# Reordering the last matrix product of a two-layer graph convolution, with its layer norms and its last bucket sums

## Chip, core and metric

One core of a Trainium2 chip. The metric is device time in microseconds (us), the median of several runs. TensorE (PE) does the matrix products, VectorE (DVE) and ScalarE (ACT) the elementwise work, GpSimd (POOL) issues the row gathers, SyncE (SP) all other transfers.

## What is computed

x is 1250 x 768; there are 21250 edges (src, dst) with one of 8 types.

```
def _rgcn_conv(x, src, dst, etype, W, root, b):
    seg = dst * num_rel + etype
    sums = segment_sum(x[src], seg)
    cnt = segment_sum(ones, seg)
    mean = (sums / maximum(cnt, 1.0)[:, None]).reshape(num_nodes, num_rel, -1)
    return einsum('nri,rio->no', mean, W) + x @ root + b

h = relu(_rgcn_conv(x, ..., W1, root1, b1))
x = layernorm(x + _rgcn_conv(h, ..., W2, root2, b2))      # eps 1e-5
```

## The kernel before

The 1250 nodes are ten **tiles** of 125 rows (T = 10). Output columns come in two **halves** of 384 (HALF). One matrix product over all nodes is called a matrix; it has 20 **steps** (STEPS), one per tile and half. A step is 18 matmuls (L720): six slices of the inner dimension times three, because each float32 operand is split into a high and a low part (high*high, high*low, low*high). In all matrices `h, t = divmod(s, T)` (L729): steps 0 to 9 do the left half of tiles 0 to 9, steps 10 to 19 the right half.

In a layer, seven relations are multiplied first and aggregated afterwards: their products go to DRAM (`y`), rows are gathered by edge (L474, POOL) and summed per destination by a matmul with a one-hot matrix (L747). A **bucket** is what the edges of one relation give for one tile of destinations; its gathered blocks are split by ACT into `g_high` (L586, L589) and by DVE into `g_low` (L986, L989), DVE builds the one-hot matrices (L978), PE multiplies, and DVE adds the result to `acc` (L997, L999). The eighth relation is averaged first and then multiplied (matrix MEAN1 in layer 1, MEAN2 in layer 2).

The change touches MEAN2, the last matrix, and what runs beside it:

- **PE** (L925, through `matrix`, L876): in each step the 18 matmuls into one of four banks (L734, after waiting for the bank: `kept`, L843), then the bucket sums that `actions(s)` names. In MEAN2 these are the ten buckets of the last relation, placed by `last_sums` (L300): tile t is summed after step 3 + 15*t//9, that is 3, 4, 6, 8, 9, 11, 13, 14, 16, 18. A bucket there is 14 matmuls, over four gathered blocks. After step 2 PE, ACT and DVE read a count of spilled edges and branch on it (L773, L665, L1053).
- **DVE** (L1356, through `matrix`, L1011): in step s it adds the product to `acc` (`keep_mean2`, L1341, operation L967); if the step has a sum, it first prepares the *next* bucket (four one-hot matrices, three `g_low`, one folded piece of 64 partitions that goes to `g_high`: L978, L986) and then adds the bucket that PE sums after this step (L997). Only bucket 0 is prepared earlier, at step 2. From step 10 on `layer_norm` (L1345) follows: statistics of tile s - 10 (L1349 to L1351), and for the tile before it the reciprocal (L1337) and the normalisation of 768 columns, `(acc - mean) * 1/std` (L1338).
- **ACT** (L701): the `g_high` of the next bucket (four of 768 columns, L586), and from step 11 on the square root of one tile's variance (`deviation`, L697), one step behind DVE's statistics.
- **POOL**: gathers of the last relation (L566). Gather i is issued when block i - 5 has been split by DVE (`low_ready`, L473), since there are five buffers `raw`. ACT writes a `g_high` slot once PE has used the block four before it (L583).
- **SP** (L423): waits for `normed` tile by tile and sends each tile of `acc` to the output (375 KiB each); nothing else is left on its queue then.

Within an engine everything is in program order, so the steps above are a schedule written out by hand.

Of the kernel before, what the change touches and what calls it, by code (L numbers as in the profile page):

```python
# [8 lines left out]
def rgcn_residual_layernorm(nc, x, src, dst, etype, w_all, b1, b2, out):  # L9
# [21 lines left out]
    R = Q // 2 - 1  # L31
    P = 128
    K = D // P
    HALF = D // 2
    T = -(-N // P)
# [31 lines left out]
    STEPS = 2 * T  # L67
# [14 lines left out]
    with ctx:  # L82
        def sb(name, shape, dt=f32):
            return ctx.enter_context(nc.sbuf_tensor(name, shape, dt))

        def sem(name):
            return ctx.enter_context(nc.semaphore(name))
# [31 lines left out]
        stats = sb("stats", [P, 2, 2, 6])  # L119
        moments = sb("moments", [P, 2, 2])  # L120
        std = sb("std", [P, 2, 2])
        spill_n = sb("spill_n", [P, 1], i32)
        spill_index = sb("spill_index", [P, 1], i32)
        spill_gid = sb("spill_gid", [P, 1])
# [97 lines left out]
        var_ready = sem("var_ready")  # L222
        std_ready = sem("std_ready")
        normed = sem("normed")
        out_stored = sem("out_stored")
        spill_copied = [sem(f"spill_copied{l}") for l in range(2)]
        spill_shifted = [sem(f"spill_shifted{l}") for l in range(2)]
# [13 lines left out]

        def unit(q, h):
            return 2 * q + h

        def behind(g):

# [42 lines left out]
        def averaging(g, r, n):  # L289
# [7 lines left out]
                return todo  # L297
            return actions

        def last_sums(g):  # L300
            return lambda s: [("sum", g, R - 1, t) for t in range(T) if s == 3 + (STEPS - 5) * t // (T - 1)]

        def sums_behind(g, s):
            return sum(len(last_sums(g)(n)) for n in range(s))
# [20 lines left out]
        def banks(shift, turning=False):  # L325
            return lambda s: 2 + s % 2 if turning and s >= T else (s + shift) % BANKS
# [5 lines left out]
        def _(sp):  # L332
# [88 lines left out]
            with sp.Fori(2, R) as r:  # L421
                relation(r + ROOT2 - 1, stored_before(1, r), r)
            for t in range(T):  # L423
                sp.wait_ge(normed, t + 1)
                sp.dma_start(out[t * NT:t * NT + ROWS[t], :], acc[0:ROWS[t], t, :]).then_inc(out_stored, 16)
            sp.wait_ge(out_stored, 16 * T)

# [142 lines left out]
        def _(act):  # L570
# [54 lines left out]
            def matrix(q, yc, bank, actions=lambda s: [], more=True, spilled=None, ahead=False, high_at=1, after=None):  # L625


                cut = SPILL_STEP[spilled[0]] if spilled else -1
                order = [(s, a) for s in range(STEPS) for a in actions(s) if a[0] != "turn"]
                ready = n = 0  # L630
                for s in range(STEPS):
                    sums = sum(a[0] != "turn" for a in actions(s))
                    turns = [a for a in actions(s) if a[0] == "turn"]
                    n += sums
                    if not ahead or ready == 0:
                        for m in range(ready, n):
                            bucket(order[m][1][1], order[m][1][3])
                        ready = n
                    if yc is not None:
                        stage_y(yc, STEPS * q + s, s, bank(s))  # L640
                    for _, turn, _, t in turns:
                        if turn == 2:
                            relu(t)
                    if ahead and sums:

                        last = min(n + 1, len(order))
                        last -= last > n and s <= cut < order[n][0]
                        for m in range(ready, last):
                            bucket(order[m][1][1], order[m][1][3])
                        ready = last  # L650
                    for _, turn, _, t in turns:
                        high_of_turn(turn, t)
                    for what, g, _, t in actions(s):
                        if what == "average":
                            average(g, t)
                    if s == high_at:
                        high_of_unit(q, 1)
                    if s == 11 and more:
                        high_of_unit(q + 1, 0)
                    if s == cut:  # L660
                        high_spilled(*spilled)
                    if after:
                        after(s)
# [33 lines left out]
            def deviation(t):  # L697
                act.wait_ge(var_ready, t + 1)
                act.activation(std[:, t % 2, 0:1], moments[:, t % 2, 1:2], ACT.Sqrt, bias=eps[:]).then_inc(std_ready, 1)

            matrix(MEAN2, None, None, finishing, more=False, spilled=(1, 2 * R - 1), ahead=True, high_at=0,  # L701
                   after=lambda s: deviation(s - T - 1) if s > T else None)
            deviation(T - 1)


        @block.tensor
        def _(pe):
# [18 lines left out]
                pe.wait_ge(w_low_ready, unit(q, h) + 1)  # L726

            def step(q, s, bank, free):
                h, t = divmod(s, T)  # L729
                if t == 0:  # L730
                    unit_ready(q, h)
                for wait in free:
                    pe.wait_ge(*wait)
                product(q, h, t, bank).then_inc(prod_done, 1)  # L734
# [108 lines left out]
            def kept(base, before, n=None, turning=False):  # L843


                def free(s):
                    wait = [(h_low_ready, 2 * T * n + 2 * s + 2)] if n is not None and s < T else []
                    if s < 2 and n is not None:
                        return wait + [(before[0], before[1] - 1 + s)]
                    if s < BANKS:  # L850
                        return wait + [(h_low_ready, 2 * T * (n + 1))]
                    return wait + [(root_kept, base + s + 1 - (2 if turning and s >= T else BANKS))]
                return free
# [76 lines left out]
        def _(dve):  # L930
# [401 lines left out]
            matrix(MEAN2 - 1, averaging(2 * R - 3, R - 2, 3), low_at=in_parts)  # L1332


            def norm(t):
                dve.wait_ge(std_ready, t + 1)
                link(dve.reciprocal(std[:, t % 2, 1:2], std[:, t % 2, 0:1]))  # L1337
                dve.tensor_scalar(acc[:, t, :], acc[:, t, :], moments[:, t % 2, 0:1], std[:, t % 2, 1:2],  # L1338
                                  ALU.subtract, ALU.mult).then_inc(normed, 1)

            def keep_mean2(s):  # L1341
                dve.wait_ge(bucket_added, 2 + T * (2 * R - 1) + sums_behind(2 * R - 1, s))
                keep(STEPS * MEAN2 + s, s % T, s // T, banks(2)(s), plus="acc")

            def layer_norm(s):  # L1345
                t = s - T
                if t >= 0:
                    dve.wait_ge(root_kept, 3 * STEPS + s + 1)
                    dve.bn_stats(stats[:, t % 2, 0, :], acc[:, t, 0:HALF])  # L1349
                    link(dve.bn_stats(stats[:, t % 2, 1, :], acc[:, t, HALF:D]))  # L1350
                    dve.bn_aggr(moments[:, t % 2, :], stats[:, t % 2].rearrange("p c s -> p (c s)"))\  # L1351
                        .then_inc(var_ready, 1)
                if t >= 1:
                    norm(t - 1)

            matrix(MEAN2, finishing, keep_mean2, more=False, spilled=(1, 2 * R - 1), after=layer_norm,  # L1356
                   low_at=((1, 0, K),))
            norm(T - 1)


# [20 lines left out]
```

## Time and profile before

| what | value |
|---|---|
| median of 3 runs | 1575.47 us (1573.15 to 1580.7) |
| profiled execution, own time | 1582.24 us |
| its span, first to last instruction | 1580.4 us |
| mean granted clock of TensorE | 0.976 |
| first matmul of MEAN2's step 3 | 1482.09 us |
| last instruction of DVE | ends 1571.14 us |

The span is the part of the profiled execution that the trace covers; all times below are counted from its start. PEld is the weight load of TensorE, which overlaps its matmuls. An arrow in brackets names what ended the idle time before an instruction.

### The profile page before, as it was taken

Reading aid. Unit: us, or ns where it says so; the run is one execution under the profiler, and the core shown is the slowest. Engines: PE = TensorE matmul, PEld = TensorE weight load, DVE = VectorE, ACT = ScalarE, POOL = GpSimd, SP = SyncE. Lnnn points to the kernel's source line nnn. Section 1 sums busy time; section 2 is a strip of 40 time slices with the busy share of each in tenths; the row PEclk is TensorE's granted clock in tenths of the full one; section 3 lists DMA queues with packets and bytes.
Section 4 is the critical chain, followed back from the end, with each engine's and each line's share of the span. In section 5 each row is a group of like instructions: output and inputs, shape, how many; then the busy total and the mean of one; then the engine's idle time right before and its main releaser. Section 6 shows DMA issues by size and latency. Waiting matters only on the chain.

```text
span 1580.4 us, 23799 instructions
## 1 busy us (share of the span) xinstructions
PE 1485.0 (94%) x9014; PEld 1462.6 (93%) x9014; DVE 1022.3 (65%) x1599; ACT 572.7 (36%) x818; POOL 629.2 (40%) x455
## 2 busy tenths in 40 slices
PE   6999998999999998999989799999999999899995
PEld 5999998999999998998989799999999999899995
DVE  6899999955777765885971022545454545478797
ACT  3222111112444543584552111333333334258542
POOL 1121112223677774664620310434343424366561
PEclk9999999999999998999999899999999999999998
DMA  4353221243677766765423441656565555576443
GB/s 163 114 189 123 83 74 34 71 140 112 190 245 218 215 206 210 221 201 160 142 85 130 150 149 42 197 157 203 167 197 172 190 182 184 171 234 202 137 138 124
DMA packets 102645, 249.79 MB, mean 158 GB/s; under 512 B 12607, under 2 KB 75758, under 8 KB 102486
## 3 DMA queue, kind: packets, MB, share of 16 engines
q0 software_dynamic: 31680, 131.81, 27.5%
q1 hardware_dynamic: 70870, 116.69, 22.2%
q8 instruction: 62, 1.02, 0.3%
q14 instruction: 33, 0.27, 0.0%
HBM read 204.47 MB, written 65.49 MB: 171 GB/s over the span
## 4 chain that ended last, share of the span: by engine, by line
PE 58%; DVE 20%; DMA 12%; POOL 4%; issue 3%; ACT 2%; SPq 0%; DVEq 0%; ACTq 0%; POOLq 0%
PE prod L720 45%; PE agg L747 11%; DMA y<-y_stage 5%; DMA raw<-y,bucket_index 5%; DVE slot_hot L1214 3%; POOL raw L474 2%; DVE ranks L1169 2%; DVE ranks L1164 2%; DVE keyed L1222 2%; POOL scale L482 1%; DVE dst_hot L1215 1%; DVE g_low L989 1%; PE prod L711 1%; DMA x_rows<-in_x 1%; DVE g_low L986 1%
## 5 line engine op out<-in xcount | busy, mean ns | idle before, releaser
L720 PE MATMUL prod<-w_high,h_high 128*128 128x384 f32 x2160 | 736.3, 341 | 20.2 <-ACT y_stage L622 12.8
L720 PE MATMUL prod<-w_low,h_high 128*128 128x384 f32 x2160 | 730.4, 338 | 0.0
L720 PE MATMUL prod<-w_high,h_low 128*128 128x384 f32 x2160 | 729.7, 338 | 0.0
L474 POOL DMA_INDIRECT raw<-y,bucket_index x380 | 492.8, 1297 | 559.5 <-DVE g_low L989 296.8
L989 DVE TENSOR_TENSOR g_low<-raw,g_high 128x768 fp32r<-128x768 f32 x280 | 259.1, 954 | 306.6 <-ACT g_high L589 305.8
L720 PEld LDWEIGHTS prod<-w_high,h_high 128*128 128x128 f32 x2160 | 412.3, 191 | 22.8 <-ACT y_stage L622 15.4
L720 PEld LDWEIGHTS prod<-w_low,h_high 128*128 128x128 f32 x2160 | 411.8, 191 | 0.0
L720 PEld LDWEIGHTS prod<-w_high,h_low 128*128 128x128 f32 x2160 | 411.5, 191 | 0.0
L622 ACT ACTIVATE y_stage<-prod 128x384 f32<-128x384 f32 x280 | 137.5, 492 | 702.4 <-PE prod L720 639.7
L589 ACT ACTIVATE g_high<-raw 128x768 fp32r<-128x768 f32 x300 | 243.2, 842 | 106.8 <-DMA raw<-y,bucket_index 87.6
L747 PE MATMUL agg<-g_high,one_hot 128*128 128x384 f32 x760 | 202.5, 348 | 22.6 <-DVE g_low L989 20.6
L747 PE MATMUL agg<-g_low,one_hot 128*128 128x384 f32 x680 | 176.2, 341 | 0.0
L747 PEld LDWEIGHTS agg<-g_high,one_hot 128*128 128x128 f32 x760 | 135.9, 190 | 33.5 <-issue 17.5
L461 POOL TENSOR_TENSOR w_low<-w_raw,w_high 128x2304 fp32r<-128x2304 f32 x8 | 58.7, 7341 | 252.4 <-ACT w_high L576 252.4
L747 PEld LDWEIGHTS agg<-g_low,one_hot 128*128 128x128 f32 x680 | 126.3, 191 | 0.0
L999 DVE SCALAR_TENSOR_TENSOR acc<-agg,inv_count,acc 128x768 f32<-128x768 f32 x120 | 121.3, 1011 | 4.4 <-PE agg L747 4.1
L945 DVE TENSOR_TENSOR w_low<-w_raw,w_high 128x2304 fp32r<-128x2304 f32 (+1 forms) x37 | 72.7, 1965 | 56.5 <-ACT w_high L576 56.5
L576 ACT ACTIVATE w_high<-w_raw 128x2304 fp32r<-128x2304 f32 x36 | 76.5, 2125 | 64.5 <-PE prod L720 46.6
L586 ACT ACTIVATE g_high<-raw,scale 128x768 fp32r<-128x768 f32 x80 | 70.8, 931 | 72.3 <-issue 39.4
L978 DVE TENSOR_SCALAR one_hot<-column,dst_local 128x128 fp32r<-128x128 bf16 x380 | 89.0, 290 | 7.5 <-issue 7.0
L967 DVE TENSOR_TENSOR acc<-prod,acc 128x384 f32<-128x384 f32 x60 | 33.2, 554 | 82.5 <-PE prod L720 81.8
L1214 DVE TENSOR_SCALAR slot_hot<-slot,edge_f 125x512 f16<-125x512 f16 x170 | 60.6, 430 | 0.0
(138 smaller groups left out, 772.1 us busy)
## 6 DMA issues: line engine op xcount, KB each, us to landing
y<-y_stage SPq DMA_DIRECT2D x280, 187.5 KB
w_raw<-in_w_all SPq DMA_DIRECT2D x36, 1152.0 KB
raw<-y,bucket_index POOLq DMA_INDIRECT x380, 5.3
x_rows<-in_x SPq DMA_DIRECT2D x10, 375.0 KB
y<-in_x SPq DMA_DIRECT2D x1, 3750.0 KB, 14.8
y<-acc SPq DMA_DIRECT2D x10, 375.0 KB
acc<-in_x SPq DMA_DIRECT2D x10, 375.0 KB
out<-acc SPq DMA_DIRECT2D x10, 375.0 KB
```

What stands on the lines that cost most here:

```text
L474: pool.indirect_dma_start(raw[:, i % NRAW, :], None, y[0:written * N, :], bass.IndirectOffsetOnAxis(ap=bucket_index[:, at_column:at_column ...
L576: act.activation(w_high[:, h], w_raw[:], ACT.Copy).then_inc(w_high_ready, 1)
L586: act.activation(g_high[:, split_slot(g, i), :], raw[:, slot, :], ACT.Copy, scale=scale[:, i:i + 1])\
L589: act.activation(g_high[:, split_slot(g, i), :], raw[:, slot, :], ACT.Copy).then_inc(high_ready, 1)
L622: act.activation(y_stage[:, s % BANKS, :], prod[:, bank, 0:HALF], ACT.Copy)\
L720: mm = pe.matmul(prod[:, bank, 0:HALF], left[:, k, t * P:(t + 1) * P], right[:, h, k, :], start=(k == 0 and left is h_high and right is w_ ...
L747: mm = pe.matmul(agg[:, par, c, 0:HALF], one_hot[:, par, b, :], part[:, split_slot(g, i), c * HALF:(c + 1) * HALF], start=(b == 0 and part ...
L945: ins = dve.tensor_tensor(w_low[:, h, part], w_raw[:, part], w_high[:, h, part].bitcast(f32), ALU.subtract)
L978: ins = dve.tensor_scalar(one_hot[:, par, b, :], column[:], dst_local[:, bass.ds(column_of(r, t, b), 1)], None, ALU.is_equal)
L989: ins = dve.tensor_tensor(low[p:P, split_slot(g, i), :], rows, high, ALU.subtract)
L999: ins = dve.scalar_tensor_tensor(a, agg[:, t % 2, :, 0:HALF], inv_count[:, bass.ds(r * T + t, 1)], a, ALU.mult, ALU.add)
L1214: dve.tensor_scalar(slot_hot[:, c % 2, j, :], slot[0:EP, :], place[:, e:e + 1], None, ALU.is_equal)
```

## The change

MEAN2 no longer does all left halves first. With LEAD = 4: steps 0 to 3 are the left halves of tiles 0 to 3, steps 4 to 7 their right halves, and from step 8 on the halves of one tile follow each other. The bucket sums of the last relation move to steps 4 + 13*t//9, which are 4, 5, 6, 8, 9, 11, 12, 14, 15, 17 (the same relation in layer 1 keeps its steps). A tile is finished at the later of its second half and its sum: steps 4, 5, 6, 8, 9, 11, 13, 15, 17, 19 for tiles 0 to 9. DVE takes the statistics in that step. ACT takes the square root in the same step (before: one step later). In the next step DVE, ahead of its addition of the product, waits for the square root, takes the reciprocal and computes `shift = -mean/std` (128 x 1), and ACT, behind its `g_high`, normalises the tile with `Identity(acc * 1/std + shift)`. Tile 9 is still normalised by DVE, under a semaphore of its own.

```
         def part_of(q, s):
+            if not (isinstance(q, int) and q == MEAN2):
+                return divmod(s, T)
+            if s < 2 * LEAD:
+                return divmod(s, LEAD)
+            return s % 2, s // 2
+
+        def finished_at(t):
+            return max(LEAD + t if t < LEAD else 2 * t + 1, last_sum_at(2 * R - 1, t))
+
+        def finished(s):
+            return [t for t in range(T) if finished_at(t) == s]
...
+        def last_sum_at(g, t):
+            first, steps = (3, STEPS - 5) if g < R else (4, 13)
+            return first + steps * t // (T - 1)
+
         def last_sums(g):
-            return lambda s: [("sum", g, R - 1, t) for t in range(T) if s == 3 + (STEPS - 5) * t // (T - 1)]
+            return lambda s: [("sum", g, R - 1, t) for t in range(T) if s == last_sum_at(g, t)]
...
-                sp.wait_ge(normed, t + 1)
+                sp.wait_ge(*((normed, t + 1) if t < T - 1 else (last_normed, 1)))
...
+            def norm(t):
+                act.wait_ge(norm_ready, t + 1)
+                act.activation(acc[:, t, :], acc[:, t, :], ACT.Identity, bias=shift[:, t % 2, :],
+                               scale=std[:, t % 2, 1:2]).then_inc(normed, 1)
+
+            def layer_norm(s):
+                for t in finished(s - 1):
+                    norm(t)
+                for t in finished(s):
+                    deviation(t)
+
             matrix(MEAN2, None, None, finishing, more=False, spilled=(1, 2 * R - 1), ahead=True, high_at=0,
-                   after=lambda s: deviation(s - T - 1) if s > T else None)
-            deviation(T - 1)
+                   after=layer_norm)
...
-                h, t = divmod(s, T)
+                h, t = part_of(q, s)
...
-                    wait = [(h_low_ready, 2 * T * n + 2 * s + 2)] if n is not None and s < T else []
+                    h, t = part_of(MEAN2 if n == 3 else None, s)
+                    wait = [(h_low_ready, 2 * T * n + 2 * t + 2)] if n is not None and h == 0 else []
...
-            def norm(t):
+            def scale_of(t):
                 dve.wait_ge(std_ready, t + 1)
                 link(dve.reciprocal(std[:, t % 2, 1:2], std[:, t % 2, 0:1]))
-                dve.tensor_scalar(acc[:, t, :], acc[:, t, :], moments[:, t % 2, 0:1], std[:, t % 2, 1:2],
-                                  ALU.subtract, ALU.mult).then_inc(normed, 1)
+                dve.tensor_scalar(shift[:, t % 2, :], moments[:, t % 2, 0:1], std[:, t % 2, 1:2], -1.0,
+                                  ALU.mult, ALU.mult).then_inc(norm_ready, 1)

             def keep_mean2(s):
+                for t in finished(s - 1):
+                    scale_of(t)
+                h, t = part_of(MEAN2, s)
                 dve.wait_ge(bucket_added, 2 + T * (2 * R - 1) + sums_behind(2 * R - 1, s))
-                keep(STEPS * MEAN2 + s, s % T, s // T, banks(2)(s), plus="acc")
-
-            def layer_norm(s):
-                t = s - T
-                if t >= 0:
+                keep(STEPS * MEAN2 + s, t, h, banks(2)(s), plus="acc")
+
+            def moments_of(s):
+                for t in finished(s):
                     dve.wait_ge(root_kept, 3 * STEPS + s + 1)
+                    dve.wait_ge(bucket_added, 2 + T * (2 * R - 1) + t + 1)
                     dve.bn_stats(stats[:, t % 2, 0, :], acc[:, t, 0:HALF])
                     link(dve.bn_stats(stats[:, t % 2, 1, :], acc[:, t, HALF:D]))
                     dve.bn_aggr(moments[:, t % 2, :], stats[:, t % 2].rearrange("p c s -> p (c s)"))\
                         .then_inc(var_ready, 1)
-                if t >= 1:
-                    norm(t - 1)
...
-            norm(T - 1)
+            last = (T - 1) % 2
+            dve.wait_ge(std_ready, T)
+            link(dve.reciprocal(std[:, last, 1:2], std[:, last, 0:1]))
+            dve.tensor_scalar(acc[:, T - 1, :], acc[:, T - 1, :], moments[:, last, 0:1], std[:, last, 1:2],
+                              ALU.subtract, ALU.mult).then_inc(last_normed, 1)
```

## Rows read from the trace of the kernel before

**Rows 1.** The page: PE's busy time, and the chain that ended last by engine.
```profile
PE 1485.0 (94%) x9014; PEld 1462.6 (93%) x9014; DVE 1022.3 (65%) x1599; ACT 572.7 (36%) x818; POOL 629.2 (40%) x455
...
PE 58%; DVE 20%; DMA 12%; POOL 4%; issue 3%; ACT 2%; SPq 0%; DVEq 0%; ACTq 0%; POOLq 0%
```

**Rows 2.** Busy time by stretch: length, then PE, PEld, DVE, ACT, POOL, clock, DMA.
```profile
1540.00:1550.00 10.00, 9.93 (x58) 9.61 (x57) 9.84 (x19) 3.83 (x5) 6.92 (x6) 1.00 0.60 176
...
1560.00:1570.00 10.00, 2.90 (x17) 2.58 (x15) 9.61 (x25) 1.18 (x4) 0.00 (x0) 0.85 0.28 97
```

**Rows 3.** Chain of waits, MEAN2 steps 3 and 4 (start, us, what).
```profile
1479.65 2.44 issue
1482.09 4.79 PE prod L720 x18
1486.88 2.46 PE agg L747 x14
1489.35 3.12 PE prod L720 x18
```

**Rows 4.** Timeline of DVE, one full step (start, us, what), and bucket 1's start.
```profile
1487.47 0.94 DVE L978 TENSOR_SCALAR one_hot<-column,dst_local 128x128 fp32r<-128x128 bf16 x4
...
1543.42 0.55 DVE L967 TENSOR_TENSOR acc<-prod,acc 128x384 f32<-128x384 f32 x1
1543.88 0.86 DVE L978 TENSOR_SCALAR one_hot<-column,dst_local 128x128 fp32r<-128x128 bf16 x4
1544.67 2.87 DVE L986 SCALAR_TENSOR_TENSOR g_low<-raw,scale,g_high 128x768 fp32r<-128x768 f32 x3
1547.57 1.02 DVE L986 SCALAR_TENSOR_TENSOR g_high<-raw,scale,g_high 64x768 fp32r<-64x768 f32 x1
1548.62 0.96 DVE L997 TENSOR_TENSOR acc<-agg,acc 128x768 f32<-128x768 f32 x1
1549.49 0.55 DVE L1349 BATCH_NORM_STATS2 stats<-acc 128x6 f32<-128x384 f32 x1
...
1550.54 0.21 DVE L1351 BATCH_NORM_AGGREGATE moments<-stats 128x2 f32<-128x12 f32 x1
1550.66 0.11 DVE L1337 RECIPROCAL std<-std 128x1 f32<-128x1 f32 x1
1550.81 0.68 DVE L1338 TENSOR_SCALAR acc<-acc,moments,std 128x768 f32<-128x768 f32 x1
1551.40 0.55 DVE L967 TENSOR_TENSOR acc<-prod,acc 128x384 f32<-128x384 f32 x1
```

**Rows 5.** Waits, 1460 to 1581: us in total, times, longest.
```profile
DVE g_low L986 <- ACT g_high L586: 1.1, 5, 0.3
```

**Rows 6.** Timeline of ACT: its square roots and what stands around them.
```profile
1528.47 1.28 ACT L699 ACT_TABLE_LOAD   x1
1529.76 0.30 ACT L699 ACTIVATE std<-moments,eps 128x1 f32<-128x1 f32 x1
...
1533.68 3.42 ACT L586 ACTIVATE g_high<-raw,scale 128x768 fp32r<-128x768 f32 x4 [1.08 <-PE agg L747]
...
1567.15 0.29 ACT L699 ACTIVATE std<-moments,eps 128x1 f32<-128x1 f32 x1 [3.07 <-DVE moments L1351]
```

**Rows 7.** Timelines: PE's last matmul; DVE's last statistics and last norm.
```profile
1562.56 0.34 PE L720 MATMUL prod<-w_high,h_low 128*128 128x384 f32 x1
...
1569.41 0.21 DVE L1351 BATCH_NORM_AGGREGATE moments<-stats 128x2 f32<-128x12 f32 x1
...
1570.46 0.68 DVE L1338 TENSOR_SCALAR acc<-acc,moments,std 128x768 f32<-128x768 f32 x1
```

**Rows 8.** By stretch, columns as in rows 2; the last is GB/s.
```profile
1563.00:1564.00 1.00, 0.00 (x0) 0.00 (x0) 0.93 (x5) 0.22 (x1) 0.00 (x0) 1.00 0.33 77
...
1567.00:1578.00 11.00, 0.00 (x0) 0.00 (x0) 3.97 (x11) 0.59 (x2) 0.00 (x0) 0.50 0.32 127
...
1579.00:1580.40 1.40, 0.00 (x0) 0.00 (x0) 0.00 (x0) 0.00 (x0) 0.00 (x0) 0.50 0.02 9
```

More of the change, by code:

```diff
@@ L121, in rgcn_residual_layernorm @@
         std = sb("std", [P, 2, 2])
+        shift = sb("shift", [P, 2, 1])
         spill_n = sb("spill_n", [P, 1], i32)
@@ L224, in rgcn_residual_layernorm @@
         normed = sem("normed")
+        last_normed = sem("last_normed")
+        norm_ready = sem("norm_ready")
         out_stored = sem("out_stored")
@@ L243, in unit, with part_of @@
             return 2 * q + h
+        LEAD = 4
+        def part_of(q, s):
+            if not (isinstance(q, int) and q == MEAN2):
[7 more added lines that the diff above has]
+            return [t for t in range(T) if finished_at(t) == s]
         def behind(g):
@@ L1352, in layer_norm @@
                         .then_inc(var_ready, 1)
-                if t >= 1:
-                    norm(t - 1)
-            matrix(MEAN2, finishing, keep_mean2, more=False, spilled=(1, 2 * R - 1), after=layer_norm,
+            matrix(MEAN2, finishing, keep_mean2, more=False, spilled=(1, 2 * R - 1), after=moments_of,
                    low_at=((1, 0, K),))
-            norm(T - 1)
+            last = (T - 1) % 2
[3 more added lines that the diff above has]
+                              ALU.subtract, ALU.mult).then_inc(last_normed, 1)
 def kernel(x, src, dst, edge_type_8, L0_gnn_W1, L0_gnn_root1, L0_gnn_b1, L0_gnn_W2, L0_gnn_root2, L0_gnn_b2):
```

## The prediction

> **What bounds the kernel now.** I read the page first. PE is busy for 94% of the span and carries 58% of the chain that ended last [rows 1]. The change touches only the last matrix, so at most the stretch from step 3 on, some 98 us of 1580, can move. There I read busy time by stretch. Around 1545 us PE and DVE are both full (9.93 and 9.84 of 10 us), and after 1560 us PE runs out of work (2.90) while DVE goes on (9.61) [rows 2]. PE's last matmul ends at 1562.90, DVE's last norm at 1571.14 [rows 7]. So the end is set by DVE, 8.2 us behind PE, and then by a tail of transfers: 1580.40 - 1571.14 = 9.26 us. The timeline of DVE shows why: a step with both a bucket and a norm takes 7.98 us from one addition of a product to the next [rows 4], while PE needs 3.12 for the product and 2.46 for the bucket, together 5.58 [rows 3].
>
> **PE's own work** doesn't change: the same products and buckets, in another order. If nothing held it, then from the end of step 3's product at 1486.88 [rows 3] it would need 16 products and ten buckets: 16 x 3.12 + 10 x 2.46 = 74.5, ending at 1561.4. That is the floor, and it is little better than the 1562.9 of now.
>
> **The price list of DVE**, by the distances between starts [rows 4]: addition of a product 0.46 (alone about 0.6), one-hot matrices 0.79, three g_low 2.90, folded piece 1.05, addition of a bucket 0.87, statistics 1.05 + 0.12, reciprocal 0.15, norm 0.59.
>
> **The norm moves to ACT.** DVE loses 0.59 per tile and gets a 128 x 1 operation; the trace has none of this kind with two operands, the nearest row is the reciprocal with 0.15 [rows 4], bounds 0.05 and 0.3. But the order adds a wait. Before, the square root of a tile was one step old when DVE asked for it. Now DVE asks at once after the statistics, and nothing stands between. Behind that wait stand DVE's addition of the next product and all the preparation of the next bucket. The square root starts when the moments are out and takes 0.29 [rows 6]; with a hop each way I take 0.36, bounds 0.29 and 0.6. So a full step goes from 7.98 to 7.98 - 0.59 + 0.15 + 0.36 = 7.90. **Nearly all that DVE gives away comes back as a wait.** ACT itself has room: 3.83 of 10 us busy [rows 2], and a norm there should cost about what a g_high of the same size costs (3.42 for four, [rows 6]), so under 1 us, bounds 0.8 and 1.1, beside DVE's g_low work.
>
> **The table load.** It stands before the first square root, 1.28 us [rows 6]. Now it came at 1528.47 while nobody waited. With tile 0 finished in step 4 it falls into the wait just described, unless it is issued ahead of it: bounds 0 and 1.28, taken 1.28, because the load stands under the line of the square root, behind its wait. The square root follows the load at once, at 1529.76 [rows 6]. The Trainium skill (ScalarE: Activation LUTs, What ACT_TABLE_LOAD costs) puts a drain of about 1.38 us beside the load; by it the end would be another 1.4 us later. The row shows no such gap before the square root.
>
> **The sums move.** The first bucket goes from step 3 to step 4. Before, DVE began bucket 1 at 1487.47, right behind step 3's product [rows 4]; now it has nothing to do until step 4's product, 1486.88 + 3.12 = 1490.0. That gives away 2.5 us of the engine that is the bound. From there DVE's order is fixed. Up to the last piece that bucket 8 needs (prepared in step 14) it does six full steps (4, 5, 6, 8, 9, 11): 47.4; step 12 without statistics: 0.46 + 0.79 + 2.90 + 1.05 + 0.87 = 6.07; steps 7 and 10, an addition each: 1.2; step 13, addition and statistics with their wait: 0.6 + 1.83 = 2.43; step 14 up to the fold: 5.20. Together 62.3. To this come the table load 1.28 and waits for g_high: 1.1 us over five now [rows 5]; ACT now starts a bucket only after the square root, so I take 0.8, bounds 0 and 2.4. Sum 64.4, so 1554.4. PE's work meanwhile (products 5 to 15, buckets 0 to 7) is 54.0, so PE is the one that waits.
>
> **The end of the chain goes back to PE.** Bucket 8 ends about 0.4 later, at 1554.8. Then products 16 and 17, 6.24: 1561.0. Bucket 9, already prepared: 1563.5. Products 18 and 19: 1569.7. Then addition 0.6, statistics 1.05, aggregate 0.21, square root 0.36, reciprocal 0.15, norm 0.68, together 3.0: **1572.8**, which is 1.6 later than now. DVE's backlog of today is gone, but PE ends 6.8 later than today.
>
> **The output tail shrinks.** Now the last tile leaves behind others: the moved rate is 127 GB/s from 1567 to 1578 [rows 8], so at 1571.14 some 0.98 MB were still to go, two and a half tiles of 0.384 MB. After the change ACT's norm of tile 8 comes at about 1568.2 (bucket 9 at 1563.5, its addition, statistics, square root, norm), 4.6 us ahead of tile 9, so tile 9 has the queue to itself. One transfer alone moves 77 GB/s [rows 8], which makes 5.0 us; with a start of under 1 us and the 1 us in which almost nothing moves at the end (9 GB/s, [rows 8]) I take 6.6, bounds 5.0 (at 127 GB/s) and 9.26. Gain 2.7. The first eight outputs move earlier too (the first to about 1504: step 4's 7.9 us after 1490, the table load, the g_high of step 5 and a norm, instead of 1533), in among the gathers; nothing is queued behind them on SP. I cost them at nothing: four of them already share the engines with gathers now (DMA share 0.60, [rows 2]). Without this cover they would lengthen gathers, which is a rival below. The wait for h_low moves with the tile and costs nothing: all turns are done before step 2.
>
> **The sum:** 1572.8 + 6.6 = 1579.4 against 1580.4, a gain of 1.0. The profiled execution took 1582.24, so it would take 1581.2; it stood 6.8 above the median of the three runs, and I subtract from that median: **1574.5 us**. A measurement of this kernel tells about 0.5%, 7.9 us, from no change, so the forecast is no measurable difference. From the bounds above: the small operation and the square root, on eight tiles, -1.4 to +3.1; table load -1.3; g_high waits -0.8 to +1.6; tail -1.6 to +2.7.
>
> **Rivals.**
>
> *DVE is really relieved.* If neither the wait for the square root nor the late start mattered, PE would run through: 1561.4 + 3.0 + 6.6 = 1571.0, a gain of 9.4, 1566.1 us. For it: DVE's total falls, and its eight full-width norms go. Against: the 7.90 of a full step stand against PE's 5.58, and four of the five steps 4 to 8 are such steps. To reach it DVE would have to be 7 us or more shorter. Chance 0.06.
>
> *Gathers get late.* The outputs from 1504 us on take part of the DMA engines while POOL's gathers need them, and each bucket's chain starts with a gather that waited for DVE. If each of the six buckets behind the first output got 1 us later and nothing absorbed it, the time would be 1580.5. For it: the DMA share is already 0.60 [rows 2]. Against: a gather's five buffers run a bucket ahead and ACT is idle 6 us in 10. Chance 0.12; still within 0.5%.
>
> *The square root and the scaling don't share a table.* Identity is not in the trace of before; if it needed another table than the square root, ACT would load at each change of function. DVE waits for the load before a square root, on tiles 1 to 6 and on tile 9: 7 x 1.28 = 9.0, ending at 1583.5, 8.0 slower than now. It decides from the second tile on, in step 5. For it: nothing beyond that the case is not shown. Against: the copy with a scale at 1533.68 follows a square root with no load [rows 6]. Chance 0.03. The Trainium skill (ScalarE: Activation LUTs, Table sets: the hidden batching unit) says that cheap functions, identity among them, are in every set; by it this rival falls.
>
> *The clock.* A gap of 2.44 us at 1479.65 is followed by a product of 4.79 instead of 3.12 [rows 3]. If DVE's longer steps open such a gap in PE, each costs up to 1.7. I expect PE's gaps in pieces under 1 us; chance 0.05 for one or two of them, 1577.
>
> **How the numbers follow.** Forecast 0.74, gathers 0.12, relieved DVE 0.06, clock 0.05, table 0.03. Around the forecast the bounds reach some 5 us either way. The range 1568 to 1580.5 takes in the forecast's bounds, the clock and the gathers' case, and leaves out most of the other two. Faster by over 0.5% (below 1567.6): the relieved DVE and a little of the forecast's low end, 0.07. Slower by over 0.5% (above 1583.3): the table rival and a part of the late gathers, 0.05. Within: 0.88.
>
> **What would show it.** Right: DVE's step with bucket and norm still near 7.9 us, with about 0.36 idle before each reciprocal that ends with ACT's square root; one table load near step 4 with DVE idle 1.5 or more; DVE idle 2.5 before step 4's addition; PE waiting for g_low in most buckets; PE's last matmul near 1570 and 3 us from there to the last norm; a tail near 6.6. Wrong: PE's last matmul before 1565 (DVE was relieved); more than two table loads; ACT waiting for gathers while DVE waits for ACT's g_high; a tail still near 9.

## The result, and the profile after

| | median us | ratio to before, 95% interval |
|---|---|---|
| before | 1577.12 | |
| changed | 1588.36 (1583.16 to 1592.6, 6 runs) | 1.0064, 1.0033 to 1.0095 |
| changed, 12 more runs, later | 1589.88 | 1.0064, 1.0042 to 1.0086 |

The last row stands beside 1579.45 for the kernel before on the same chip. The change makes the kernel 10 us slower. I had forecast no difference, 1574.5 us, with 1580.5 as the upper end of the range. One of the 12 executions of a kernel below (e4) ran at a mean granted clock of 0.79 and took 1743.68 us; it stands in no ratio.

The profiled execution of the changed kernel has a span of 1581.4 us, 1.0 longer than that of before. Single executions of one kernel differ by several us ahead of the last matrix: over all 20 profiles of this study its step 3 begins between 1475.9 and 1489.9 us. So I compare the **last stage**, from the start of step 3's product to the end of the span. The page after (busy time; the chain by engine):

```profile
PE 1484.4 (94%) x9014; PEld 1460.1 (92%) x9014; DVE 1021.0 (65%) x1599; ACT 579.7 (37%) x827; POOL 626.8 (40%) x455
...
PE 60%; DVE 19%; DMA 14%; issue 3%; ACT 2%; POOL 2%; SPq 0%; DVEq 0%; ACTq 0%; POOLq 0%
```

The chain of waits of the changed kernel in that stage (start, us, what):

```profile
1478.70 6.50 PE prod L754 x36
1485.20 2.49 PE agg L781 x14
...
1499.46 7.43 DMA raw<-y,bucket_index
...
1528.34 6.51 DMA raw<-y,bucket_index
...
1544.28 7.68 DMA raw<-y,bucket_index
...
1555.72 6.27 PE prod L754 x36
1561.99 2.48 PE agg L781 x14
1564.47 6.26 PE prod L754 x36
```

Steps 3 and 4 lie back to back, then the chain leaves PE and runs over DVE, ACT and gathers of 6.5 to 7.7 us, and from 1555.72 on it is PE again: two products, bucket 9, two products, as predicted.

The timeline of DVE, one step with bucket and norm, as [rows 4]:

```profile
1521.99 0.55 DVE L1002 TENSOR_TENSOR acc<-prod,acc 128x384 f32<-128x384 f32 x1
1522.45 0.86 DVE L1013 TENSOR_SCALAR one_hot<-column,dst_local 128x128 fp32r<-128x128 bf16 x4
1523.24 2.87 DVE L1021 SCALAR_TENSOR_TENSOR g_low<-raw,scale,g_high 128x768 fp32r<-128x768 f32 x3
1526.14 1.02 DVE L1021 SCALAR_TENSOR_TENSOR g_high<-raw,scale,g_high 64x768 fp32r<-64x768 f32 x1
1527.19 0.96 DVE L1032 TENSOR_TENSOR acc<-agg,acc 128x768 f32<-128x768 f32 x1
1528.25 0.56 DVE L1387 BATCH_NORM_STATS2 stats<-acc 128x6 f32<-128x384 f32 x1
...
1529.31 0.21 DVE L1389 BATCH_NORM_AGGREGATE moments<-stats 128x2 f32<-128x12 f32 x1
1529.88 0.16 DVE L1372 RECIPROCAL std<-std 128x1 f32<-128x1 f32 x1 [0.36 <-ACT std L723]
1530.08 0.21 DVE L1373 TENSOR_SCALAR shift<-moments,std 128x1 f32<-128x1 f32 x1
1530.21 1.01 DVE L1002 TENSOR_TENSOR acc<-prod,acc 128x384 f32<-128x384 f32 x2
```

From one addition to the next it is 8.22 us, against 7.98 before: the wait of 0.36 stands ahead of the reciprocal, reciprocal and shift take 0.33 together, and the statistics begin 1.06 behind the start of the bucket's addition instead of 0.87, since they now need the sum just made. (Where they need an older sum, for tile 7 at 1563.97, it is 0.87 in this kernel too.)

The waits from 1460 us on, as [rows 5] (total, times, longest):

```profile
ACT g_high L610 <- DMA raw<-y,bucket_index: 15.0, 9, 3.3
PE agg L781 <- DVE g_low L1021: 8.5, 7, 2.4
DVE g_low L1021 <- ACT g_high L610: 5.4, 8, 1.4
...
DVE std L1372 <- ACT std L723: 3.3, 9, 0.4
...
DVE g_high L1021 <- ACT g_high L610: 1.8, 1, 1.8
```

The timeline of ACT, as [rows 6]: the table load runs ahead of the wait of the square root it serves (it ends at 1491.59, the square root is released at 1494.44), so it costs nothing.

```profile
1490.31 1.28 ACT L723 ACT_TABLE_LOAD   x1
1494.44 0.30 ACT L723 ACTIVATE std<-moments,eps 128x1 f32<-128x1 f32 x1 [2.84 <-DVE moments L1389]
...
1497.95 1.02 ACT L727 ACTIVATE acc<-acc,shift,std 128x768 f32<-128x768 f32 x1
```

And DVE's last instruction, as [rows 7] (the span ends at 1581.4):

```profile
1573.24 0.68 DVE L1397 TENSOR_SCALAR acc<-acc,moments,std 128x768 f32<-128x768 f32 x1
```

Counted from the start of step 3's product, so that the kernels can be laid beside each other (worked out from the timelines, one profile each, two where two numbers stand; the tail is the time from the end of the last norm to the end of the span):

| kernel | PE's last matmul | last norm | tail | stage |
|---|---|---|---|---|
| before | 80.8 / 79.5 | 89.1 / 87.8 | 9.3 / 9.2 | 98.3 / 97.0 |
| forecast | 87.6 | 90.7 | 6.6 | 97.3 |
| changed | 92.0 / 91.6 | 95.2 / 94.8 | 7.4 / 6.6 | 102.7 / 101.4 |

One part of these stages has nothing to do with the schedule. From the start of step 3's product to the start of what follows, PE takes 3.2 us in 16 of the 20 profiles, and 4.6 to 5.9 in the other four: the first one of before, and below the two kernels with the sums at 3 (a2, f1) and b2. The granted clock of TensorE is lower there. By stretch, columns as in [rows 2], first before, then changed:

```profile
1482.10:1485.10 3.00, 3.00 (x9) 3.00 (x10) 2.97 (x4) 1.61 (x2) 1.69 (x2) 0.50 0.50 135
```
```profile
1478.90:1481.90 3.00, 3.00 (x18) 3.00 (x18) 2.26 (x4) 1.67 (x2) 2.39 (x3) 1.00 0.31 86
```

Behind this product the stage takes 93.7 and 93.8 us before and 99.4 and 98.1 changed; the forecast comes to 92.7. So the stage loses 4.4 us from its start, or 5.7 and 4.4 behind the product. That is about half of the 10 that the times show; the experiments had to find both parts.

### The profile page after: what moved, and what is told of

Its sections match the earlier page's. It is cut to its first block, busy times and chain, and to the rows that moved or that the text cites. A ratio compares the mean times of both kernels' runs of the same rounds, so it can differ in the third digit from the quotient of the medians.

```text
span 1581.4 us, 23818 instructions
## 1 busy us (share of the span) xinstructions
PE 1484.4 (94%) x9014; PEld 1460.1 (92%) x9014; DVE 1021.0 (65%) x1599; ACT 579.7 (37%) x827; POOL 626.8 (40%) x455
## 3 DMA queue, kind: packets, MB, share of 16 engines
q8 instruction: 62, 1.02, 0.3%
## 4 chain that ended last, share of the span: by engine, by line
PE 60%; DVE 19%; DMA 14%; issue 3%; ACT 2%; POOL 2%; SPq 0%; DVEq 0%; ACTq 0%; POOLq 0%
PE prod L754 47%; PE agg L781 11%; DMA y<-y_stage 6%; DMA raw<-y,bucket_index 5%; DVE slot_hot L1249 3%; DMA x_rows<-in_x 2%; DVE ranks L1204 2%; DVE ranks L1199 2%; DVE keyed L1257 2%; DVE g_low L1021 2%; DVE dst_hot L1250 1%; DVE g_low L1024 1%; POOL raw L498 1%; PE prod L745 1%; DVE ranks L1191 1%
## 5 line engine op out<-in xcount | busy, mean ns | idle before, releaser
L613 ACT ACTIVATE g_high<-raw 128x768 fp32r<-128x768 f32 x300 | 242.2, 841 | 96.9 <-DMA raw<-y,bucket_index 79.2
L1021 DVE SCALAR_TENSOR_TENSOR g_low<-raw,scale,g_high 128x768 fp32r<-128x768 f32 x60 | 58.2, 1014 | 8.3 <-ACT g_high L610 8.3
```

Source lines behind the costliest of these rows:

```text
L613: act.activation(g_high[:, split_slot(g, i), :], raw[:, slot, :], ACT.Copy).then_inc(high_ready, 1)
L1021: ins = dve.scalar_tensor_tensor(low[p:P, split_slot(g, i), :], rows, scale[p:P, i:i + 1], high, ALU.mult, ALU.subtract)
```

## The experiments

Each kernel ran 12 times (the held outputs 11) beside 23 to 35 executions of the kernel before on the same chip. The ratio of one kernel to before is told to about 0.2%, 3 us; the difference of two such ratios only to about 0.3%, 5 us. *Stage* is counted from the start of step 3's product, *behind the product* from the start of what follows it. Each run has a short name, in brackets where it is introduced; in front of each result stands what I expected, as put down before the run.

### Where in the schedule

**The changed kernel again** (a0).

> The changed kernel once more, for a second profile and more times. All theories expect some 10 us over the kernel before, since its six times lay there. What it tells apart: the one profile of the changed kernel (1583.16 us) was its fastest run, and in it the last stage (from step 3's product to the end) had 102.7 us against 98.3 before. If the loss is made in the last stage and varies with the gathers, this profile shows a stage nearer 105 to 108 us with longer waits of DVE for ScalarE's g_high; if it is made elsewhere, the stage is again near 103 us and the span is longer ahead of it.

Measured: 1.0064 (1.0042 to 1.0086), stage 101.4. The waits repeat (DVE for g_high 4.8 us, nine waits of 0.36). The stage is not near 105, so the profiles leave some 5 us of the loss unexplained.

**Outputs held back** (a1).

```
             for t in range(T):
+                if t == 0:
+                    sp.wait_ge(normed, 5)
```

> Changed kernel, but SyncE sends no output before tile 4 is normalised (about where the kernel before sent its first one). Theory contention (the early outputs make gathers late): the waits of DVE for g_high (5.4 us in the profile of the changed kernel) fall to about 1 us and the time falls by 4 us or more. Theory schedule (DVE's late start, the wait for the square root and PE's end cause the loss): no change of the waits, time within 1 us of the changed kernel, or up to 3 us longer because more outputs queue at the end.

Measured: 1.0068 (1.0046 to 1.0091), stage 106.7. The first output leaves at 1532.09, and DVE waits longer for g_high, not less:

```profile
ACT g_high L612 <- DMA raw<-y,bucket_index: 17.2, 9, 4.8
DVE g_low L1023 <- ACT g_high L612: 9.4, 8, 4.0
```

PE's last matmul comes at 93.8, the tail grows to 9.6. Contention of the early outputs with the gathers falls as the cause of the waits and of the loss.

**The two parts of the schedule**, undone one at a time: the sums stay at steps 3 + 15t//9 (a2); or `scale_of`, which waits for the square root, moves behind DVE's addition and its bucket work (a3, "asks later"):

```
-            first, steps = (3, STEPS - 5) if g < R else (4, 13)
+            first, steps = (3, STEPS - 5)
```
```
             def keep_mean2(s):
-                for t in finished(s - 1):
-                    scale_of(t)
...
             def moments_of(s):
+                for t in finished(s - 1):
+                    scale_of(t)
```

> Changed kernel, but the last bucket sums stay at the steps of before (3 + 15t//9). Theory schedule: DVE starts bucket 1 one product (3 us) earlier and three full steps in a row fall apart, so 4 to 5 us faster than the changed kernel. Theory contention: the outputs still leave among the gathers, so at most 1 to 2 us faster.

> Changed kernel, but DVE asks for the square root at the end of the next step (after its bucket work) and not ahead of its next addition, so that nothing waits for ScalarE's square root. Theory schedule: the nine waits of 0.36 us go, 2 to 3 us faster. Theory contention: outputs leave 7 us later each, otherwise the same; no more than 1 us.

Measured, sums at 3: 1.0012 (0.9991 to 1.0033), stage 97.3. Asks later: 1.0027 (1.0002 to 1.0052), stage 96.9. Against 1.0064 that is some 8 and 6 us, each told to about 5, where I had expected 4 to 5 and 2 to 3. The stages gain 4.7 and 5.1; behind the product they take 92.5 and 93.7, against 93.7 of before. So either repair brings the stage back to that of before. The time with the sums at 3 is not clear of no change, the other is just clear of it. That hints at a loss outside the stage, and no more than hints.

### What lies outside the stage

**The kernel before again** (b0).

> The kernel before once more, for a second profile of it. In its first profile step 3 of the last matrix began at 1482.1 us and the stage from there to the end took 98.3; the changed kernel and its three variants began it at 1477.6 to 1485.7 and took 102.7 and 101.4 (changed kernel, two profiles), 106.7, 97.4 and 96.9. If the whole loss lies in the last stage, this profile begins the stage within that band and takes 95 to 98. If some 5 us are lost ahead of it, the stage begins at 1474 to 1477 here.

Measured: 1.0007 (0.9987 to 1.0027), stage 97.0 from 1482.8 on. So the starts in the profiles don't show a loss ahead of the stage.

**Only the new tile and the two semaphores, unused, in the kernel before** (b1):

```
         std = sb("std", [P, 2, 2])
+        shift = sb("shift", [P, 2, 1])
...
         normed = sem("normed")
+        last_normed = sem("last_normed")
+        norm_ready = sem("norm_ready")
```

> The kernel before with only the new tile (shift, 8 bytes per partition) and the two new semaphores, unused. Theory schedule: no change, within 2 us of before. Rival, layout: the new tile moves every tile behind it and the semaphores their numbers; if that costs time anywhere in the 1480 us ahead, this one is 4 us or more slower than before.

Measured: 1.0043 (1.0023 to 1.0064), 6.8 us, for a program that does nothing new. **The theory of the schedule alone falls.** Split in two, only the tile (d1) and only the semaphores (d2):

> The kernel before with only the new tile of 8 bytes, unused. The tile and the two semaphores together cost 0.43% (6.8 us). If the tile does it (it moves the small tiles behind it by 8 bytes; the large region stays where it was, since its start is rounded up), 5 to 7 us slower than before; if the semaphores do it, no change.

> The kernel before with only the two new semaphores, unused, in the middle of the list. If the semaphores' numbers do it, 5 to 7 us slower than before; if the tile does it, no change. If both of these two runs show no change, the 6.8 us were chance or need both.

Measured: tile 1.0033 (1.0014 to 1.0053), semaphores 0.9994 (0.9973 to 1.0015). It is the tile. Its 8 bytes per partition move the ten small tiles allocated behind it; by the sizes in the code, packed one behind another, the large region with `acc`, `raw`, `g_high` and `g_low` keeps its place. Two more unused tiles tell something about which places matter: 64 bytes instead of 8 (e2), and the 8 bytes further back, ahead of `small` (e4).

> The kernel before with an unused tile of 64 bytes instead of 8 in the same place, so that every tile behind it keeps its address modulo 64. If the 8 bytes cost because they put later tiles off an alignment, no change; if any shift costs (or what sits at the end of the memory), 5 us slower as with 8 bytes.

> The kernel before with the unused 8 bytes placed later, ahead of the tile 'small', so that only small, small_bf and over_bf move. If these are the tiles that mind, 5 us slower as with the tile in its place; if the edge tiles (payload, position, dl_bf, key_bf) do, no change.

Measured, 64 bytes: 1.0013 (0.9988 to 1.0038), which is not clear of no change, nor of the 8 bytes' effect (by the same sizes this one moves the large region too, by 64 bytes). 8 bytes ahead of `small`, moving only `small`, `small_bf` and `over_bf`: 1.0034 (1.0009 to 1.0059). So moving these three tiles is enough. **What in it costs is open**: they are used only in the first 430 us, where each DVE operation on them takes the same in either layout within what one layout varies by itself, and step 3 of the last matrix begins at 1482.4 on average over ten profiles without the 8 bytes and at 1483.0 over ten with them, each scattering by over 3. A part may lie in the last stage, where none of the three is used: behind step 3's product it takes 95.8, 95.7 and 95.6 us in the kernels with the unused 8 bytes, 93.7 and 93.8 in before and 94.7 with only the semaphores, one profile each. But with the 64 bytes it takes 95.4.

### The schedule without the tile's cost

The tile goes behind all others, and the semaphores to the end of the list (cut, the semaphores are left out):

```
-        shift = sb("shift", [P, 2, 1])
...
         base = -(-top // 32) * 32
+        shift = sb("shift", [P, 2, 1])
```

This is the changed kernel in that form (d3):

> The changed kernel, all of its schedule, but the new tile is placed behind all others and the new semaphores at the end of the list, so that everything of before keeps its place. Theory layout plus schedule: 5 us or more faster than the changed kernel, 3 to 5 us slower than before, which is what the last stage shows in the profiles (102.7 and 101.4 us against 98.3 and 97.0). Theory schedule alone: still 10 us slower than before.

Measured: 1.0038 (1.0017 to 1.0058). The schedule costs 6 us; the rest, 4 us between 1.0064 and 1.0038, is not told from nothing by this pair alone. PE waits 9.3 us for g_low, and DVE 4.7 us for the g_high that its g_low needs, as in the changed kernel.

And its two parts undone as above, one at a time (f1, f2) and both (e1):

> Changed kernel with the last sums at their steps of before and the tiles in their old places; DVE still waits for the square root. In the new layout it stood 0.12% over before (last stage 97.3 us), so with the tile's 0.3% gone 3 us faster than before; both repairs together gave 0.33% faster in the old layout. If it lies near 0, the wait for the square root is worth 3 to 5 us by itself.

> Changed kernel with the square root asked for later and the tiles in their old places; the sums stay at steps 4 + 13t//9. In the new layout it stood 0.27% over before (last stage 96.9 us), so with the tile's 0.3% gone 0 to 1 us faster than before. If it lies as low as both repairs together (0.33% faster), the move of the sums costs only where DVE also waits for the square root.

> Changed kernel with both repairs (last sums at their steps of before, square root asked for later) and the old places of all tiles. Its last stage was 96.0 us with the new layout, against 97 to 99 for the kernel before; with the tile's 5 us gone it should be 1 to 3 us faster than before, which five rounds may not tell from nothing. If it is still 3 us or more slower, the layout is not what the earlier run of it paid.

| schedule, old places | ratio | 95% interval | last norm | stage | behind the product |
|---|---|---|---|---|---|
| as changed (d3) | 1.0038 | 1.0017 to 1.0058 | 98.5 | 104.7 | 101.5 |
| sums at 3 (f1) | 1.0006 | 0.9991 to 1.0021 | 92.2 | 98.4 | 92.5 |
| asks later (f2) | 1.0010 | 0.9992 to 1.0028 | 91.1 | 97.6 | 94.3 |
| both (e1) | 0.9967 | 0.9949 to 0.9985 | 88.1 | 94.6 | 91.4 |

The stage of d3 is 2.0 us longer than the changed kernel's for a reason of its own: bucket 8 and the product behind it take 9.6 us there against 7.7, and the granted clock from 1557.4 to 1564.0 us is 0.57.

In these times the two losses add up: 0.32% and 0.28% alone, 0.71% together. With both repaired **the kernel is 0.33% faster than before**, 5 us, the best of this study. Its timeline of DVE has no wait ahead of a reciprocal except tile 9's. At 1511.62, in a step without a bucket:

```profile
1510.00 0.55 DVE L1387 BATCH_NORM_STATS2 stats<-acc 128x6 f32<-128x384 f32 x1
...
1511.05 0.21 DVE L1389 BATCH_NORM_AGGREGATE moments<-stats 128x2 f32<-128x12 f32 x1
1511.18 0.51 DVE L1002 TENSOR_TENSOR acc<-prod,acc 128x384 f32<-128x384 f32 x1
1511.62 0.16 DVE L1372 RECIPROCAL std<-std 128x1 f32<-128x1 f32 x1
1511.82 0.22 DVE L1373 TENSOR_SCALAR shift<-moments,std 128x1 f32<-128x1 f32 x1
```

The square root now runs beside the next addition, and in a step with a bucket beside the bucket work too. What the repairs did not take away are DVE's waits for g_high: 5.6 us, against 5.4 and 4.8 in the changed kernel. What fell are PE's waits for g_low, from 9.3 in d3:

```profile
DVE g_low L1021 <- ACT g_high L610: 5.6, 8, 1.7
...
PE agg L781 <- DVE g_low L1021: 2.9, 2, 2.4
```

The same schedule as e1 with the tile in its new place (b2):

> Changed kernel with both repairs: last sums at their steps of before, and DVE asking for the square root one step's work later. Measured alone they gave 8.9 and 6.4 us. If they are two losses that add up, 1575 or less and faster than before; if both act on the same thing (buckets too close together for their gathers), about 1580, no faster than the better one alone.

Measured: 1.0018 (0.9996 to 1.0041), stage 96.0. Beside e1 it is the tile that keeps this kernel from being faster than before. It does not explain why the repairs fail to add up here, 0.52% and 0.37% alone and 0.46% together, since the tile has the same place in all four. Behind the product they overlap in both layouts: 9.0 and 7.1 us alone against 10.1 together in the old places, 6.3 and 5.1 against 7.6 in the new. **Whether these are two losses or partly one is not settled.**

Four schedules have now run with the tile in both places. The new place costs 0.26% (as changed), 0.06% (sums at 3), 0.17% (asks later) and 0.51% (both), on average 0.25%.

### One part at a time

**Only the order of the product** (b3): sums at 3, and DVE normalises as before.

> Only the order of the product and of the layer norms is changed: last sums at the steps of before, DVE normalises all 768 columns itself one step behind. Against b2 it shows what the norm on ScalarE is worth when nothing waits for it: 9 x 0.59 less 9 x 0.3, about 2.5 us, so this one 2 to 3 us slower than b2. Against before it shows what the order is worth: layer norms of early tiles beside PE's work, 3 to 5 us faster if DVE is the bound of the stage.

Measured: 1.0025 (1.0004 to 1.0047) with the tile in its new place, stage 96.1, last norm 88.9, tail 7.2. Against b2 (1.0018) the times tell no worth of the norm on ScalarE. Behind the product the stage takes 92.9 here and 91.2 in b2, 1.7 us for it, in one profile each; from the stage's start it was hidden by b2's slow first product.

**Only the sums moved** (c1), in the kernel before.

> The kernel before with only the last bucket sums moved to steps 4 + 13t//9; product order, norms and layout as before. Theory schedule: DVE starts bucket 1 a product later and PE's end comes behind two products after the last bucket, so 3 to 5 us slower, with the last stage at 101 to 103 us. If the sums cost only together with the norms in the same steps, no change here.

Measured: 1.0019 (1.0000 to 1.0038), stage 98.3, last norm 88.6. Behind the product the profile shows a loss of 1.3 us (95.1 against 93.7 and 93.8, but 94.7 with only the semaphores added), the times perhaps 3: moved alone, the sums cost little. I put that down to the norms, which here still stand in steps 10 to 19; no run shows it.

**Only the norm on ScalarE** (e3), in the old places.

> Old product order, old steps of the sums, old places of the tiles; only the norm goes to ScalarE, with its wait for the square root ahead of DVE's next addition, as in the changed kernel. Theory schedule: what DVE gives (0.59 a tile) it gets back in waits (0.36 + 0.33 measured for the two small operations and the hop), so last stage within 1 us of before, less 2 to 3 us at the end since the outputs queue no longer.

Measured: 1.0014 (0.9994 to 1.0033), no change that can be told. PE's last matmul comes at 84.7 instead of 80.8, the last norm at 92.8 instead of 89.1, and the tail is 7.5 instead of 9.3. So the last norm is about 4 us later in this profile, and the shorter queue of outputs gives half of it back. But most of the 4 us is one wait for g_high, and ACT stood idle for a gather then (timelines of DVE and of ACT):

```profile
1551.58 1.02 DVE L1017 SCALAR_TENSOR_TENSOR g_low<-raw,scale,g_high 128x768 fp32r<-128x768 f32 x1 [3.30 <-ACT g_high L606]
```
```profile
1550.62 1.76 ACT L606 ACTIVATE g_high<-raw,scale 128x768 fp32r<-128x768 f32 x2 [3.38 <-DMA raw<-y,bucket_index]
```

Whether the norm on ScalarE made that gather late is not shown.

## Why the prediction was wrong

**It missed a rival.** I listed four ways for it to go and none was the new tile itself. Its declaration, the first line that the change adds to the kernel, was read as costing nothing and was not priced at all. It costs 0.33 to 0.43% in the three kernels that have an unused tile and no new work, some 5 to 7 us, and 0.06 to 0.51% in the four schedules. With it alone added, my forecast would have been about 1580, and the measured 1588 would still lie above.

**The term of the sum that was mis-sized is DVE's stretch from step 4's addition to the last piece of bucket 8.** I had 64.4; it was 69.8 (1485.31 to 1555.07 in the changed kernel). The other terms moved the stage less: its start -1.3 (step 3's product ran at the higher clock), PE's end +0.4, the last norm +0.1, the tail +0.8; together they make the 5.4 between 97.3 and 102.7. The stretch by its parts:

- *The full step:* 7.90 forecast, 8.22 measured where nothing else waits, six times 0.3, about 2. The wait of 0.36 was right. What I missed is that the statistics now wait for the sum of the same step (0.19), and that with nothing behind it the aggregate counts with its whole 0.21 instead of 0.12.
- *Waits for g_high:* 0.8 forecast, bounds up to 2.4; about 4.5 measured in this stretch, of the 5.4 in the whole stage. This is the largest part, 3.7 us. I took them from five waits of before [rows 5], and that profile was the lowest of all: the nine profiles in which DVE does the norm have 1.1 to 3.9 us of them ahead of `g_low` in the stage, the eleven with the norm on ScalarE 3.5 to 5.9, and 9.4 with the outputs held. So the price was too low even for kernels without the hand-over. ACT in turn waits for gathers (11.7 us in the stage, 15.0 from 1460 on), and POOL issues a gather only when DVE has split the block five before it.
- *The table load:* 1.28 forecast, 0 measured; the load stands ahead of the wait. The Trainium skill's drain of 1.38 us beside the load (ScalarE: Activation LUTs, What ACT_TABLE_LOAD costs) can't be seen here either: ACT was idle for 2.84 us behind it, which would hide one.
- *A first step of 9.8* instead of 7.9: 0.9 of it are waits for g_high, counted above (ScalarE's second g_high of bucket 1 had to wait 0.77 for PE's bucket 0), and 0.48 is a wait ahead of the first statistics.

**What held.** DVE is the bound in the middle, and what the norm gave it comes back as the round trip (0.59 against 0.36 and 0.33); the end goes to PE, two products, a bucket, two products: 15.3 forecast, 15.7 measured from bucket 8's last piece; last norm 3.2 behind PE instead of 3.0; the tail 6.6 forecast, 7.4 and 6.6 measured, against 9.26. A norm on ScalarE took 1.02 against my "under 1", within its bounds. Some signs that I had listed need care. PE's last matmul "near 1570" came at 1570.72 and the profiled execution at 1583.16 against 1581.2, but that is luck: step 3 began 3.4 us earlier than in the profile that I had counted from. DVE's idle 2.5 ahead of step 4's addition was 0.5 and, in the second profile, 1.3. And one sign of being wrong stood in both profiles: ACT waits for gathers while DVE waits for ACT's g_high.

**The rivals.** DVE relieved: no, its step got longer. Late gathers: the waits came, but not by the cause I gave, for with the outputs held back they stayed. I gave this 0.12 and a price of 6 over the forecast, by a mechanism that this run refutes. What makes the waits long stays open. That the buckets follow each other too closely does not fit: undoing either part of the schedule brought the stage back, but left waits of 3.5 to 5.9 us, 5.6 in the fastest kernel. No table was loaded a second time, as the Trainium skill's rule on cheap functions has it (the same page, Table sets: the hidden batching unit). The clock: one stretch shows 0.83 (1510 to 1520 us), against 1.00 in the neighbouring ones. I had expected gaps of PE in pieces under 1 us; here one of 2.42 us ends at 1516.18, and the bucket behind it takes 4.23 instead of 2.64. It cost the changed kernel nothing on the chain, for DVE never waited for a bucket in this stage. In d3 the clock was low in the end that belongs to PE, and there it cost 2.0 us.

```profile
1510.00:1520.00 10.00, 7.56 (x33) 7.19 (x34) 9.12 (x17) 4.63 (x6) 5.05 (x4) 0.83 0.53 169
```

## What to carry to other kernels

A diff is priced from its first line: an allocation in the middle of a list moves everything behind it, and a kernel of before with only the declarations added is a cheap control. When work is handed to another engine, look at what stands between the request and the use: a round trip with nothing in between gave back what the hand-over saved. Asking later removed those waits, but only together with the old places of the sums did the kernel become faster than before. A wait read from one profile is no price: here it was the lowest of twenty. And before two stages are compared, look at the granted clock of their first product, which alone made up to 2.7 us.

## What was not expected of the hardware

Eight unused bytes per partition ahead of small tiles made the kernel 0.33%, 0.34% and (with two semaphores) 0.43% slower in 12 runs each (11 for the 0.34%); in the case of 0.34% the tiles behind it are used only in the first third of the kernel. Two unused semaphores did nothing that can be told (0.9994). The reason was not found. Where DVE's statistics wait on its own addition of a bucket just made, they start 1.06 us behind its start, and 0.87 where they need an older sum. The gap of PE ahead of step 3 does not by its length decide the clock behind it: the four slow products follow gaps of 2.05 to 2.84 us, the sixteen others gaps of 1.39 to 2.87.
